# Unread products on TensorE around two waits, and four low weight parts moved from VectorE to GpSimd

## The chip, the cores and the metric

The kernel runs on one NeuronCore of a Trainium2 chip. The metric is the device time of one launch in microseconds, the median over runs. The engines are TensorE (PE, with its weight loads as PEld), VectorE (DVE), ScalarE (ACT), GpSimd (POOL) and SyncE (SP), which here only issues transfers. Each runs its own list of instructions in order; semaphores tie them together.

## The reference

The input is x of 4 batches by 512 tokens by 512 channels, in float32, and per batch a vector c.

```python
mod = silu(c) @ wmod                  # six rows: sa, ca, ga, sb, cb, gb
ga, gb = clamp_away_from_zero(ga), clamp_away_from_zero(gb)
h = layernorm(x) * (1 + ca) + sa
# mixer: causal depthwise convolution, B, C and delta projections,
# a linear scan over the 512 tokens with 128 states, output projection
x = x + ga * mixer(h)
h = layernorm(x) * (1 + cb) + sb
# experts: one of 2 for each token, the larger router logit wins
e = argmax(h @ w_router.T); p = softmax(h @ w_router.T)[e]
a = square(where(u >= 0, u, 0.5 * u)),  u = h @ w_fc[e].T    # 2048 hidden
x = x + gb * p * (a @ w_proj[e].T)
```

## The kernel before

**Mixer stage.** The batches b = 0 to 3 are worked through one after the other in a pipeline, with the order of every engine written out by hand. For each batch TensorE transposes the normalized rows (`transposes1`, L930, four column blocks k into two banks in turn), multiplies them by the delta, C, B and state weights (L937, L943, L951, L961) and makes the output (L978, L982). ScalarE normalizes, modulates (`modulate1`, L651, writes hT), adds the last tap of the convolution (L659) and takes the exponentials (eabs, L667 and L669). VectorE does the rest of the convolution (L1267), softplus, the scan, the residual and the statistics. Float32 products run on TensorE in full precision. Before all this TensorE multiplies the first modulation rows (`mod_rows`, L900) and turns them into columns by tiny transposes (`turn`, L916), and at the very start it runs two products of `ident` and `eabs` into the bank `pC` that nobody reads (L1013).

**Sorting.** While the mixer runs, each token gets a place in a list sorted by expert. VectorE finds the mask `m1` (L1343), TensorE counts with it (`prefix`, L987 and L988, two products of four columns), VectorE turns the counts into ranks, offsets and one-hot permutations (L1349 to L1362), GpSimd into positions (`positions`, L542 and L543, posI), and TensorE permutes the normalized tokens (`permuted_block`, L1006). ScalarE places each permuted block into the sorted activations (`place`, L729); of the last batch VectorE places a second copy (`place_from_back`, L1547). For the last batch (b = 3) there is no next batch whose products could stand between: TensorE has `permuted_block` of batch 2, then `prefix(3)`.

**Expert stage.** The 17 blocks of 128 sorted rows form five units of 4, 4, 4, 3 and 2 blocks. The hidden dimension is cut into eight parts hb; for each, TensorE computes for each unit the first product (`first_fc`, L1093, and `fc`, L1114) and the projection (`proj`, L1140). Both are split into a high and a low part in a faster float32 format: hi x hi, hi x lo and lo x hi are summed. So each weight chunk c (0 to 7 of each hb, 128x512; 0 to 3 for the first product, 4 to 7 for the projection) needs Whi (a copy on ScalarE, `split_first` L708 for hb = 0) and Wlo = raw - Whi, one subtraction of two SBUF tiles. The activations need XShi (ScalarE, `high_rows`, L819) and XSlo = XSfull - XShi (VectorE, `low_rows`, L1536, four operations for each unit, again with two SBUF inputs). Wlo comes from GpSimd (`low`, L547) for all chunks but the first four, which VectorE computes (`lows`, L1434). GpSimd waits for these before its first.

`first_fc` runs unit 0 in three passes: pass 0 (Whi, XShi), then the four permuted blocks of batch 3, then pass 1 (Whi, XSlo; it waits for the XSlo of each k) and pass 2 (Wlo, XShi; it waits for s_wlo >= 4). Then unit 1, all three passes.

Around the first expert products the orders are:

- VectorE: ranks(3), permutations(3), low_rows(0), lows(0 to 3), assign_rest (L1399 to L1404), low_rows(1), place_from_back(0 and 1), twice (L1554), place_from_back(2 and 3), alo (L1560).
- ScalarE: high_rows(0) and (1), margin_exp(3), place(3, blocks 0 and 1), split_first(4 to 7), the relu of unit 0 (L842), place(3, blocks 2 and 3), ahi and a_full (L851, L852).
- GpSimd: positions(3), the low parts 4 to 7, then the scatter of the sorted rows' metadata (L564).
- TensorE: first_fc of units 0 and 1, then `proj` of unit 0, which waits for alo.
- SyncE: loads the next raw weights when both s_whi and s_wlo have passed the chunks that they overwrite.

Of the kernel before, what the change touches and what calls it, by code (L numbers as in the profile page):

```python
# [17 lines left out]
F32 = mybir.dt.float32  # L18
# [3 lines left out]
ALU = mybir.AluOpType  # L22
# [25 lines left out]
CH = 8  # L48
# [48 lines left out]
def wait(eng, sem, count):  # L97

    if isinstance(count, int) and count <= 0:
        return  # L100
    eng.wait_ge(sem, count)


def build(nc, x, cT, wmod, wx, win, wout, conv_w, conv_b, A_log, Dvec, router_rows, wffn, out):
    with ExitStack() as ctx:
        base = (nc.sbuf_base + 63) // 64 * 64

        def at(name, shape, dt, offset):
            return nc.alloc_sbuf_tensor_at(name, shape, dt, offset=base + offset)

        def sem(name):
            return ctx.enter_context(nc.semaphore(name))
# [14 lines left out]
        raw = at("raw", [P, CH, 512], F32, o_raw)  # L127
        Whi = at("Whi", [P, 2, CH, 512], F32R, o_whi)
        Wlo = at("Wlo", [P, 2, CH, 512], F32R, o_wlo)
# [28 lines left out]
        def take(name, shape, dt=F32):  # L158
            o = cur[0]
            cur[0] += (int(np.prod(shape[1:])) * 4 + 31) // 32 * 32  # L160
            assert cur[0] <= limit[0], (name, cur[0] - limit[0])
            return at(name, shape, dt, o)
# [8 lines left out]
        eabs = take("eabs", [P, L])  # L171
# [26 lines left out]
        wout_sb = const("wout_sb", [P, DM])  # L198
        ident = const("ident", [P, P])
# [82 lines left out]
        pB, pC, pD, pX = bank[2:6]  # L282
# [105 lines left out]
        s_whi = sem("weights_hi_ready")  # L388
        s_wlo = sem("weights_lo_ready")
# [101 lines left out]
        def _(pool):  # L491
# [47 lines left out]
            def positions(b):  # L539
                pool.wait_ge(s_rk, b + 1)  # L540
                own.settle()
                own.link(pool.tensor_tensor(posF[:, :], pos[:, :], rank[:, :], ALU.subtract))  # L542
                pool.tensor_copy(posI[:, b % 2, :], posF[:, :]).then_inc(s_pos, 1)  # L543
# [6 lines left out]
            for b in range(NB):  # L550
                wait(pool, s_sc2[b % 2], 16 * TJ * (b // 2))
                pool.tensor_copy(meta[:, b % 2, :, 1:3].bitcast(I32), tokbat[:, TJ * b:TJ * b + TJ, :]).then_inc(s_tid, 1)
                candidates(b)
                positions(b)
                if b == NB - 1:

                    pool.wait_ge(s_wlo, CH // 2)
                    for c in range(CH // 2, CH):
                        low(0, c)
                pool.wait_ge(s_pos, b + 1)  # L560
                pool.wait_ge(s_tw, b + 1)
                pool.wait_ge(s_tid, b + 1)
                for j in range(TJ):
                    pool.indirect_dma_start(out=meta_dram, out_offset=bass.IndirectOffsetOnAxis(ap=posI[:, b % 2, j:j + 1], axis=0),  # L564
                                            in_=meta[:, b % 2, j, :], in_offset=None).then_inc(s_sc2[b % 2], 16)
# [322 lines left out]
        def _(pe):  # L888
# [15 lines left out]
            def turn(r):  # L904

                if r == 2:
                    pe.wait_ge(s_gar, 1)
                else:
                    pe.wait_ge(s_rw[r], 1)
                if r < 3:  # L910

                    wait(pe, s_cols, r)
                for k in range(KT):
                    o = KT * NB * (r % 3) + NB * k
                    row = gate_row if r == 2 else mod_row[r % 2]
                    mm = pe.transpose(col_bank[r][:, o:o + NB], row[:, P * k:P * k + P], ident[0:NB, 0:NB])  # L916
                mm.then_inc(s_mc, 1)

            def transposes1(b, ks=range(KT)):
                for k in ks:  # L920

                    wait(pe, s_e0, KT * (TJ * (b - 3) + k + 1))
                    if b == 2 and k < 2:

                        pe.wait_ge(s_cols, 3 + k)
                    wait(pe, s_hT, KT * b + k - 1)
                    for j in range(TJ):
                        if k == 0:
                            pe.wait_ge(s_z, TJ * b + j + 1)
                        mm = pe.transpose(pT[k % 2][:, P * j:P * j + P], z[b][:, j, P * k:P * k + P], ident[:, :])  # L930
                    mm.then_inc(s_zT, 1)

            def delta_product(b):
                wait(pe, s_dl, b)
                for k in range(KT):
                    pe.wait_ge(s_hT, KT * b + k + 1)
                    mm = pe.matmul(pD[:, :], wdb[:, k, :], hT[b % 2][:, k, PAD:PAD + L], start=(k == 0), stop=(k == KT - 1))  # L937
                mm.then_inc(s_pd, 1)
# [45 lines left out]
            def prefix(b):  # L984
                pe.wait_ge(s_m1, b + 1)
                pe.wait_ge(s_x2, TJ * (b + 1))
                pe.matmul(pO[0][:, 0:TJ], before[:, :], m1[:, :], start=True, stop=True).then_inc(s_pf, 1)  # L987
                pe.matmul(pO[0][:, TJ:2 * TJ], ones[:, :], m1[:, :], start=True, stop=True).then_inc(s_pf, 1)  # L988

            def permuted_block(b, j):  # L990
# [15 lines left out]
                    mm = pe.transpose(place_bank[b][j][:, P * k:P * k + P], z2[:, j, P * k:P * k + P], perm[:, j, :])  # L1006
                mm.then_inc(s_pz, 1)


            pe.wait_ge(s_const, 9)  # L1010
            pe.wait_ge(s_dconst, 1)
            for n in range(2):
                pe.matmul(pC[:, :], ident[:, :], eabs[:, :], start=True, stop=True)  # L1013
            pe.wait_ge(s_silu, 1)
            mod_rows(0)
            mod_rows(1)
            turn(0)
            transposes1(0, (0, 1))
            turn(1)
            transposes1(0, (2, 3))  # L1020
            pe.wait_ge(s_wdb, 1)
            delta_product(0)
# [7 lines left out]
            for b in range(NB):  # L1030
                nxt = b + 1 < NB
                for j in ORDER[:3]:
                    skip_product(b, j)
                if b == 0:
                    skip_product(b, 0)
                pe.wait_ge(s_hm, b + 1)
                pe.wait_ge(s_wg, b + 1)
                for j in ORDER[:3]:
                    state_output(b, j)
                if not nxt:  # L1040
                    permuted_block(b - 1, 0)
                    permuted_block(b - 1, 1)
                if b > 0:
                    skip_product(b, 0)
                state_output(b, 0)
                if not nxt:
                    permuted_block(b - 1, 2)
                    permuted_block(b - 1, 3)
                if b == 0:
                    delta_product(1)  # L1050
                    mod_rows(3)
                    mod_rows(4)
                    turn(3)
                elif nxt:
                    permuted_block(b - 1, 0)
                    permuted_block(b - 1, 1)
                if nxt:
                    C_product(b + 1)
                if b == 0:
                    turn(4)  # L1060
                if b == 1:
                    transposes1(b + 2, (0, 1))
                if nxt:
                    B_product(b + 1)
                if b == 0:
                    transposes1(b + 2, (0, 1))
                if b > 0 and nxt:
                    permuted_block(b - 1, 2)
                    permuted_block(b - 1, 3)
                if b == 2:  # L1070
                    mod_rows(5)
                if nxt:
                    state_product(b + 1)
                if b + 2 < NB:
                    transposes1(b + 2, (2, 3))
                    delta_product(b + 2)
                prefix(b)
            PARTS = ((0, 0), (0, 1), (1, 0))
            W, XS, A = (Whi, Wlo), (XShi, XSlo), (ahi, alo)

            def first_fc(u, parts):

                def body(e):
                    for n in parts:
                        wp, xp = PARTS[n]
                        if n == 2:
# [17 lines left out]
            def fc(par, hb, u):  # L1104
                i, w = NU * hb + u, P * UNITS[u]

                def body(pieces):
                    for m in range(HM):
                        for c0, c1, e in pieces:
                            n = 0  # L1110
                            for k in range(KT):
                                for wp, xp in PARTS:
                                    o = HB * (k % 2) + P * m
# [19 lines left out]
            def proj(par, hb, u):  # L1133
                i = NU * hb + u

                def body(experts):
                    for m in range(HM):
                        for s in range(UNITS[u]):
                            for n, (ap, wp) in enumerate(PARTS):
                                mm = pe.matmul(yP[s][:, :], A[ap][:, m, P * s:P * s + P], W[wp][:, par, 4 + 2 * experts[s] + m, :],  # L1140
# [82 lines left out]
        def _(dve):  # L1223
# [204 lines left out]
                dve.wait_ge(s_gbc, 16 * NB)  # L1428
                dve.tensor_tensor(woutg[b][:, :], wout_sb[:, :], ga_bc[:, b, :], ALU.mult).then_inc(s_wg, 1)

            def lows(cs):
                for c in cs:
                    dve.wait_ge(s_whi, c + 1)
                    dve.tensor_tensor(Wlo[:, 0, c, :], raw[:, c, :], Whi[:, 0, c, :].bitcast(F32), ALU.subtract).then_inc(s_wlo, 1)  # L1434

            own.mark(dve.memset(ones[:, :], 1.0))
            own.mark(dve.memset(run[:, :], 0.0))
            own.mark(dve.memset(hT[0][:, :, 0:PAD], 0.0))
# [44 lines left out]
            for b in range(NB):  # L1483
                nxt = b + 1 < NB
# [104 lines left out]
            ranks(NB - 1)  # L1589
            permutations(NB - 1)  # L1590
            low_rows(0)
            lows(range(4))
            assign_rest()
            low_rows(1)
            dve.wait_ge(s_e1, TJ * (NB - 1))
# [81 lines left out]
```

## Time and profile before

| | us |
|---|---|
| three runs | 555.43, 552.07, 554.42 |
| median | 554.42 |
| the profiled execution's own time | 554.07 |
| its span | 552.2 |

| engine | busy, us | share of the span |
|---|---|---|
| TensorE products | 508.4 | 92% |
| TensorE weight loads | 387.2 | 70% |
| VectorE | 345.8 | 63% |
| ScalarE | 261.2 | 47% |
| GpSimd | 149.8 | 27% |

The span is what the profiler recorded between the first and the last instruction; the time has 1.87 us more around it. All times of rows are from that one execution, counted from the start of its span. The mixer stage fills the first 150 us, the expert stage the rest. In the timeline a row is: start, length, engine, line, operation, output<-inputs, shape, count, and in brackets the idle time of that engine before it with what ended it. Float32 products appear as two records each (x8 is four products); records of one row overlap by a little, so a row's length over its count is not the time between starts. In the window rows stand the stretch, its length, TensorE's busy time and records in it, the granted clock as a share of 2.4 GHz (0.50 is 1.2 GHz; a value between means that the clock changed within the stretch), and the DMA engines' busy share with what they moved. In the chain's row "issue" is time in which the engine waited for nothing that the profile shows.

### The profile page before, as it was taken

Reading aid. Unit: us, or ns where it says so; the run is one execution under the profiler, and the core shown is the slowest. Engines: PE = TensorE matmul, PEld = TensorE weight load, DVE = VectorE, ACT = ScalarE, POOL = GpSimd, SP = SyncE. Lnnn points to the kernel's source line nnn. Section 1 sums busy time; section 2 is a strip of 40 time slices with the busy share of each in tenths; the row PEclk is TensorE's granted clock in tenths of the full one; section 3 lists DMA queues with packets and bytes.
Section 4 is the critical chain, followed back from the end, with each engine's and each line's share of the span. In section 5 each row is a group of like instructions: output and inputs, shape, how many; then the busy total and the mean of one; then the engine's idle time right before and its main releaser. Section 6 shows DMA issues by size and latency. Waiting matters only on the chain.

```text
span 552.2 us, 7695 instructions
## 1 busy us (share of the span) xinstructions
PE 508.4 (92%) x2280; PEld 387.2 (70%) x2280; DVE 345.8 (63%) x725; ACT 261.2 (47%) x520; POOL 149.8 (27%) x195
## 2 busy tenths in 40 slices
PE   6899899999388999999999999999999999999960
PEld 1345355544276888898888888889888888888840
DVE  4488999899999674554454545446444545446780
ACT  1664377957677633443443353344344335332310
POOL 1100003030335510330240042033015003734883
PEclk9899999999779999999999999999999999999995
DMA  8930351220043004220021022003002200344995
GB/s 303 425 113 0 113 194 57 97 77 2 1 129 103 4 3 154 69 87 1 1 87 69 1 78 78 1 23 134 1 1 77 78 2 0 85 112 93 155 125 66
DMA packets 15008, 44.19 MB, mean 80 GB/s; under 512 B 5016, under 2 KB 5016, under 8 KB 11624
## 3 DMA queue, kind: packets, MB, share of 16 engines
q1 hardware_dynamic: 10600, 34.71, 17.7%
q0 software_dynamic: 4352, 8.69, 8.9%
q8 instruction: 40, 0.66, 0.5%
q14 instruction: 16, 0.13, 0.1%
HBM read 34.94 MB, written 8.71 MB: 79 GB/s over the span
## 4 chain that ended last, share of the span: by engine, by line
PE 71%; DVE 17%; ACT 4%; issue 3%; DMA 1%; POOL 1%; ACTq 1%; SPq 0%; DVEq 0%; POOLq 0%
PE bank L1140 33%; PE bank L1114 32%; DVE xc L1267 4%; ACT XSfull L729 2%; DVE res L1305 2%; PE bank L937 1%; DVE st L1312 1%; DMA x_in<-x 1%; DVE st L1249 1%; POOL out L598 1%; DVE eabs L1329 1%; PE bank L1093 1%; DVE hs L1295 1%; PE bank L951 1%; PE bank L961 1%
## 5 line engine op out<-in xcount | busy, mean ns | idle before, releaser
L547 POOL TENSOR_TENSOR Wlo<-raw,Whi (+1 forms) x60 | 76.2, 1300 | 233.8 <-ACT Whi L857 225.2
L1570 DVE TENSOR_TENSOR acc<-acc,bank 128x512 f32<-128x512 f32 x119 | 81.2, 687 | 62.6 <-PE bank L1140 62.6
L1554 DVE TENSOR_TENSOR twice_h<-twice_h,bank 128x512 f32<-128x512 f32 (+2 forms) x80 | 48.1, 606 | 99.2 <-ACT twice_h L842 99.2
L1140 PE MATMUL bank<-Whi,ahi 128*128 128x512 f32 x272 | 106.1, 390 | 3.7 <-DVE alo L1560 3.7
L1114 PE MATMUL bank<-XShi,Wlo 128*128 x304 | 108.1, 355 | 0.0
L1114 PE MATMUL bank<-XSlo,Whi 128*128 x304 | 108.0, 355 | 0.0
L1114 PE MATMUL bank<-XShi,Whi 128*128 x304 | 108.0, 355 | 0.0
L1140 PE MATMUL bank<-Wlo,ahi 128*128 128x512 f32 x272 | 106.1, 390 | 0.0
L1140 PE MATMUL bank<-Whi,alo 128*128 128x512 f32 x272 | 106.0, 390 | 0.0
L851 ACT ACTIVATE ahi<-twice_h 128x512 fp32r<-128x512 f32 (+2 forms) x80 | 45.5, 568 | 120.3 <-PE bank L1140 120.3
L842 ACT ACTIVATE twice_h<-bank 128x512 f32<-128x512 f32 (+2 forms) x80 | 42.2, 531 | 87.0 <-PE bank L1114 77.7
L1114 PEld LDWEIGHTS bank<-XShi,Whi 128*128 128x128 f32 x304 | 57.3, 189 | 7.5
L1114 PEld LDWEIGHTS bank<-XSlo,Whi 128*128 128x128 f32 x304 | 57.3, 188 | 7.5
L1114 PEld LDWEIGHTS bank<-XShi,Wlo 128*128 128x128 f32 x304 | 57.3, 189 | 6.9
L1140 PEld LDWEIGHTS bank<-Whi,ahi 128*128 128x128 f32 x272 | 51.1, 188 | 14.6 <-issue 4.5
L1140 PEld LDWEIGHTS bank<-Whi,alo 128*128 128x128 f32 x272 | 51.1, 188 | 10.7
L1140 PEld LDWEIGHTS bank<-Wlo,ahi 128*128 128x128 f32 x272 | 51.1, 188 | 10.1
L1560 DVE TENSOR_TENSOR alo<-a_full,ahi 128x512 fp32r<-128x512 f32 (+2 forms) x80 | 46.2, 607 | 0.0
L852 ACT ACTIVATE a_full<-twice_h 128x512 f32<-128x512 f32 (+2 forms) x80 | 44.2, 552 | 0.0
L1267 DVE SCALAR_TENSOR_TENSOR xc<-hT,cw,xc 128x512 f32<-128x512 f32 x48 | 33.6, 743 | 1.8 <-ACT xc L659 1.4
L729 ACT ACTIVATE XSfull<-bank,cols 128x128 f32 (+1 forms) x64 | 24.1, 457 | 17.1 <-PE bank L1006 15.4
L598 POOL DMA_INDIRECT out<-acc,sorted_meta x17 | 28.2, 1659 | 12.2 <-DVE acc L1578 8.2
(182 smaller groups left out, 552.3 us busy)
## 6 DMA issues: line engine op xcount, KB each, us to landing
raw<-wffn SPq DMA_DIRECT2D x16, 1024.0 KB, 5.2
wm<-wmod SPq DMA_DIRECT2D x6, 1024.0 KB, 12.5
out<-res SPq DMA_DIRECT2D x4, 1024.0 KB, 4.5
x_in<-x SPq DMA_DIRECT2D x3, 1024.0 KB, 12.4
ga_bc<-ga_rows SPq DMA_DIRECT2D x4, 256.0 KB, 3.7
x<-x SPq DMA_DIRECT2D x1, 1024.0 KB, 5.3
bc<-router_rows_scaled SPq DMA_DIRECT2D x4, 256.0 KB, 3.5
wx_sb<-wx SPq DMA_DIRECT2D x1, 514.0 KB, 8.5
```

The source lines that it names most:

```text
L547: pool.tensor_tensor(Wlo[:, hb % 2, c, :], raw[:, c, :], Whi[:, hb % 2, c, :].bitcast(F32), ALU.subtract).then_inc(s_wlo, 1)
L598: pool.indirect_dma_start(out=out, out_offset=bass.IndirectOffsetOnAxis(ap=sorted_meta[:, n, 1:2].bitcast(I32), axis=0), in_=acc[:, n, :], ...
L729: act.activation(XSfull[:, k, bass.ds(first, P)], place_bank[b][j][:, P * k:P * k + P], ACT.Identity, bias=cols[:, 4, k, b:b + 1], scale=c ...
L842: act.activation(twice_h[:, m, 0:w], hP[(par + u) % 2][m][:, 0:w], ACT.Relu).then_inc(s_relu[m], 1)
L851: act.activation(ahi[:, m, 0:w], twice_h[:, m, 0:w], ACT.Square, scale=0.5).then_inc(s_ah[m], 1)
L852: act.activation(a_full[:, m, 0:w], twice_h[:, m, 0:w], ACT.Square, scale=0.5).then_inc(s_af[m], 1)
L1114: mm = pe.matmul(hP[(par + u) % 2][m][:, c0:c1], W[wp][:, par, 2 * e + k // 2, o:o + P], XS[xp][:, k, bass.ds(start_row[u] + c0, c1 - c0)] ...
L1140: mm = pe.matmul(yP[s][:, :], A[ap][:, m, P * s:P * s + P], W[wp][:, par, 4 + 2 * experts[s] + m, :], start=(m == 0 and n == 0), stop=(m = ...
L1267: ins = dve.scalar_tensor_tensor(xc[:, b % 2, k, :], hT[b % 2][:, k, tap:tap + L], cw[:, k, tap:tap + 1], xc[:, b % 2, k, :], ALU.mult, AL ...
L1554: dve.tensor_tensor(twice_h[:, m, 0:w], twice_h[:, m, 0:w], hP[(par + u) % 2][m][:, 0:w], ALU.add).then_inc(s_q2[m], 1)
L1560: dve.tensor_tensor(alo[:, m, 0:w], a_full[:, m, 0:w], ahi[:, m, 0:w].bitcast(F32), ALU.subtract).then_inc(s_al2[m], 1)
L1570: dve.tensor_tensor(acc[:, n, :], acc[:, n, :], yP[s][:, :], ALU.add).then_inc(s_yu, 1)
```

## The change

Three edits. TensorE gets a helper `idle_products(n, operand)` that multiplies `ident` by an operand of 512 columns into the bank `pC`, which nobody reads; the two such products at the start now use it. One product is added between turn(1) and the transposes of columns 2 and 3 of batch 0, four before and two behind the prefix counts of the last batch. And VectorE's four low parts of the first expert weights (`lows`) are gone: GpSimd computes all eight, right behind positions(3), without its wait for VectorE's.

```diff
--- before.py
+++ after.py
@@ -553,9 +553,7 @@
                 candidates(b)
                 positions(b)
                 if b == NB - 1:
-
-                    pool.wait_ge(s_wlo, CH // 2)
-                    for c in range(CH // 2, CH):
+                    for c in range(CH):
                         low(0, c)
                 pool.wait_ge(s_pos, b + 1)
                 pool.wait_ge(s_tw, b + 1)
@@ -1006,17 +1004,21 @@
                     mm = pe.transpose(place_bank[b][j][:, P * k:P * k + P], z2[:, j, P * k:P * k + P], perm[:, j, :])
                 mm.then_inc(s_pz, 1)
 
+            def idle_products(n, operand):
+
+                for _ in range(n):
+                    pe.matmul(pC[:, :], ident[:, :], operand[:, :], start=True, stop=True)
 
             pe.wait_ge(s_const, 9)
             pe.wait_ge(s_dconst, 1)
-            for n in range(2):
-                pe.matmul(pC[:, :], ident[:, :], eabs[:, :], start=True, stop=True)
+            idle_products(2, eabs)
             pe.wait_ge(s_silu, 1)
             mod_rows(0)
             mod_rows(1)
             turn(0)
             transposes1(0, (0, 1))
             turn(1)
+            idle_products(1, eabs)
             transposes1(0, (2, 3))
             pe.wait_ge(s_wdb, 1)
             delta_product(0)
@@ -1074,7 +1076,11 @@
                 if b + 2 < NB:
                     transposes1(b + 2, (2, 3))
                     delta_product(b + 2)
+                if not nxt:
+                    idle_products(4, wout_sb)
                 prefix(b)
+                if not nxt:
+                    idle_products(2, wout_sb)
             PARTS = ((0, 0), (0, 1), (1, 0))
             W, XS, A = (Whi, Wlo), (XShi, XSlo), (ahi, alo)
 
@@ -1427,11 +1433,6 @@
             def out_weights(b):
                 dve.wait_ge(s_gbc, 16 * NB)
                 dve.tensor_tensor(woutg[b][:, :], wout_sb[:, :], ga_bc[:, b, :], ALU.mult).then_inc(s_wg, 1)
-
-            def lows(cs):
-                for c in cs:
-                    dve.wait_ge(s_whi, c + 1)
-                    dve.tensor_tensor(Wlo[:, 0, c, :], raw[:, c, :], Whi[:, 0, c, :].bitcast(F32), ALU.subtract).then_inc(s_wlo, 1)
 
             own.mark(dve.memset(ones[:, :], 1.0))
             own.mark(dve.memset(run[:, :], 0.0))
@@ -1589,7 +1590,6 @@
             ranks(NB - 1)
             permutations(NB - 1)
             low_rows(0)
-            lows(range(4))
             assign_rest()
             low_rows(1)
             dve.wait_ge(s_e1, TJ * (NB - 1))
```

## Rows read from the trace of the kernel before

**Rows 1.** The chain that ended last, by engine.

```profile
PE 71%; DVE 17%; ACT 4%; issue 3%; DMA 1%; POOL 1%; ACTq 1%; SPq 0%; DVEq 0%; POOLq 0%
```

**Rows 2.** Timeline of TensorE, first stretch.

```profile
17.38 0.40 PE L916 MATMUL bank<-ident,mod_row 4*128 4x4 f32 x4
18.87 1.78 PE L930 MATMUL bank<-ident,z 128*128 128x128 f32 x8 [1.08 <-ACT hT L651]
20.44 4.80 PE L937 MATMUL bank<-hT,wdb 128*128 128x512 f32 x8
...
49.02 3.60 PE L937 MATMUL bank<-hT,wdb 128*128 128x512 f32 x8
```

**Rows 3.** Windows: PE busy (x), PEclk, DMA share, GB/s.

```profile
145.50:146.00 0.50, 0.00 (x0) 0.73 0.00 0
159.00:159.50 0.50, 0.50 (x4) 0.61 0.68 82
...
19.40:19.60 0.20, 0.19 (x3) 0.60 1.07 451
...
22.80:23.00 0.20, 0.20 (x2) 0.87 1.08 451
```

**Rows 4.** Timeline of ScalarE, first stretch.

```profile
22.11 1.52 ACT L659 ACTIVATE xc<-hT,cb,cw 128x512 f32<-128x512 f32 x2
25.28 0.60 ACT L667 ACTIVATE eabs<-bank 128x512 f32<-128x512 f32 x1 [1.65 <-PE bank L937]
```

**Rows 5.** Timeline of TensorE, start of the expert stage.

```profile
149.85 0.59 PE L987 MATMUL bank<-m,before 128*128 128x4 f32 x2 [6.59 <-DVE m L1343]
...
153.26 3.77 PE L1093 MATMUL bank<-XShi,Whi 128*128 x8 [2.39 <-ACT XShi L819]
156.84 3.16 PE L1006 MATMUL bank<-perm,z 128*128 128x128 f32 x16
...
163.49 1.98 PE L1093 MATMUL bank<-XShi,Whi 128*128 x8
...
171.09 0.50 PE L1140 MATMUL bank<-Whi,ahi 128*128 128x512 f32 x1 [2.00 <-DVE alo L1560]
```

**Rows 6.** Timeline of ScalarE, start of the expert stage.

```profile
158.02 1.50 ACT L729 ACTIVATE XSfull<-bank,cols 128x128 f32 x4 [2.24 <-PE bank L1006]
...
161.11 2.20 ACT L708 ACTIVATE Whi<-raw 128x512 fp32r<-128x512 f32 x4
...
166.37 1.51 ACT L729 ACTIVATE XSfull<-bank,cols 128x128 f32 x4 [0.20 <-ACT XSfull L729]
```

**Rows 7.** Timeline of VectorE, start of the expert stage.

```profile
153.49 2.50 DVE L1536 TENSOR_TENSOR XSlo<-XSfull,XShi  x4
155.91 2.49 DVE L1434 TENSOR_TENSOR Wlo<-raw,Whi 128x512 fp32r<-128x512 f32 x4
...
159.84 2.50 DVE L1536 TENSOR_TENSOR XSlo<-XSfull,XShi  x4 [0.54 <-issue]
...
168.02 1.37 DVE L1547 TENSOR_SCALAR XSfull<-bank,cols 128x128 f32 x4 [0.34 <-ACT XSfull L729]
169.31 1.36 DVE L1560 TENSOR_TENSOR alo<-a_full,ahi 128x512 fp32r<-128x512 f32 x2
```

**Rows 8.** Timeline of GpSimd, its last positions.

```profile
153.00 0.29 POOL L543 CAST posI<-posF 128x4 int32<-128x4 f32 x1
```

**Rows 9.** Timeline, narrow windows: XSlo (VectorE) and low parts (GpSimd) at one time.

```profile
161.89 1.60 POOL L547 TENSOR_TENSOR Wlo<-raw,Whi 128x512 fp32r<-128x512 f32 x1 [8.60 <-ACT Whi L708]
...
182.78 1.30 POOL L547 TENSOR_TENSOR Wlo<-raw,Whi  x1
...
183.71 0.79 DVE L1536 TENSOR_TENSOR XSlo<-XSfull,XShi  x1
...
193.66 1.47 POOL L547 TENSOR_TENSOR Wlo<-raw,Whi  x1
...
193.90 1.51 DVE L1536 TENSOR_TENSOR XSlo<-XSfull,XShi  x1
```

## Prediction

> **What bounds the kernel now.** First the page's chain that ended last [rows 1]: TensorE holds 71% of it and VectorE 17%. From 171.09 us on TensorE computes the expert products with hardly a gap, so what can be won lies before that point: whatever moves the first projection product (L1140, 171.09) moves the end by as much. So I read the two stretches that the change touches, engine by engine in the timeline, and the granted clock in narrow windows over them.
>
> The first transposes [rows 2]: after the small transposes of L916 (until 17.8) TensorE waits 1.08 us for hT. At about 19.44 its clock falls to 1.2 GHz and is back at 2.4 GHz at about 22.85 [rows 3]. In that time the delta product takes 4.80 us; the same product at 2.4 GHz takes 3.60. ScalarE waits for it: its row of eabs shows 1.65 us idle [rows 4].
>
> The last prefix count [rows 5]: TensorE idles 6.59 us before it, the clock falls at about 145.7 and returns only at about 159.4 [rows 3]. So the eight products of L1093 at 153.26 take 3.77 us (eight like them take 1.98 at 2.4 GHz, at 163.49), and the 16 transposes of L1006 take 3.16 us. ScalarE places the first block at 158.02 after 2.24 us idle, and then works nearly without a wait to 167.88 [rows 6]. VectorE waits 0.34 us for that at 168.02, ends alo at 170.67 [rows 7], and TensorE goes on at 171.09, after 2.00 us idle. VectorE is the second bound of this stretch: from 153.49 to 170.67 it waits for little but that 0.34.
>
> **Part one, one product between turn(1) and the second pair of transposes.** It costs about 0.9 us at 2.4 GHz (3.60 for four [rows 2]), starts at 17.8 and ends at 18.7, before 18.87, so it is hidden by the wait for hT; were the clock low already it would take 1.8 and cost 0.7. I take it that the clock then holds. The delta product is then bound by ScalarE's last two hT pieces, ends near 23.4, and eabs starts when ScalarE has finished its last taps, 23.65 instead of 25.28. VectorE had been waiting for eabs too, so everything behind moves: **-1.6 us**. Ends: +0.7 and -1.6 (ScalarE is busy until 23.63 [rows 4], more can't come).
>
> **Part two, four products before and two after the last prefix count.** The last transposes end at 143.27, so the four take until 146.8 at 2.4 GHz; 3.0 us of waiting are left. m1 comes from VectorE at 149.8, so nothing waits for them (at 1.2 GHz they would end 0.3 us past it, and VectorE fills that time with z2 before it reads the counts). The clock held over the 2.00 us before 171.09 and fell within the 6.59 us; 3.0 us and the small counts lie between. I expect a fall, but a return several us before 159.4, since TensorE is then busy from 149.85 on. The two products behind the count end at 152.2 at 2.4 GHz, or 154.3 at 1.2 GHz, 1.05 us past the 153.26 at which XShi is there. Placement on ScalarE could so start between 156.0 (its own end of high_rows and the margin's exponential) and 159.1, against 158.02; I take 157.0. By itself, with the placement as the bound, this would be worth -1.0 us, ends -2.0 and +1.05. It decides nothing if the next part is as I think.
>
> **Part three, the first four low parts on GpSimd.** Removed from VectorE: 2.49 us at 155.91 [rows 7]. Added on GpSimd: four of 1.29 us. GpSimd is free after posI at 153.29 [rows 8] and the Whi that they need was split before the count, so they start at about 153.33, beside VectorE's XSlo rows (four of 0.68 us, 153.49 to 155.99), and not alone. What happens then the trace shows in three places [rows 9]:
> - VectorE's XSlo at 183.71 (384 columns; the next one took 0.55) took 0.79 and ended at 184.50, 0.42 after GpSimd's low part had ended at 184.08.
> - XSlo at 193.90 (256 columns, 0.41 alone) took 1.51: it sat through GpSimd's whole low part of 193.66 to 195.13 and ended 0.28 after it. That low part had itself taken 1.47.
> - GpSimd's low part at 161.89 took 1.60 beside the fourth XSlo of unit 1, which ended at about 162.34; without one it takes 1.29.
>
> So operations with two SBUF inputs on the two engines run one after the other, in turns, and each starts 0.13 us before the other's recorded end (195.41-0.41=195.00 against 195.13; 163.49-1.29=162.20 against 162.34). A turn of one low part and one XSlo of 512 columns is thus 1.29+0.68-2x0.13=1.71 us, where an XSlo alone follows the last in 0.60. First batch: the first low part ends 154.62, the first XSlo 155.17, the fourth 155.17+3x1.71=**160.3** instead of 155.99. The low parts are ready at 159.75, so it is XSlo that TensorE waits for. It needs 13 more products of 0.23: h is ready at 163.4, about as before, whatever part two gained.
>
> VectorE then needs 1.44 us (assign_rest and the load of a register, 158.40 to 159.84 in rows 7) and begins XSlo of unit 1 at 161.7 instead of 159.84. GpSimd's other four low parts started at 161.89, when only the last XSlo was left; they follow ScalarE's Whi at 161.11 [rows 6], with part two a little earlier, so at 160.9. Now all four XSlo meet them: the first ends 162.7 (162.2-0.13+0.68), the fourth 162.7+3x1.71=**167.9** instead of 162.34.
>
> From there VectorE had 8.33 us to the end of alo, 0.3 of it waits: 167.9+8.0=175.9, and TensorE's first projection 0.4 later, 176.3 instead of 171.09: **+5.2 us**. Ends: if the engines don't get into each other's way, VectorE gains 2.5, ScalarE's placement is the bound and this part costs 0; if each waits for the other's recorded end the turn is 1.97, and eight turns make it +7.3. I take the middle value, since three overlaps of three fit it.
>
> The Trainium skill ("SBUF — State Buffer", section on who interferes with whom) has this as a rule: a VectorE instruction with two SBUF inputs contends with a GpSimd one that reads SBUF, and the one that issues later blocks for the whole instruction. Taken literally it gives the turn of 1.97 us and a time 2.1 us above mine; the rows above show the 0.13 us of overlap, so the measurement decides.
>
> **The clock behind it.** TensorE ends the products of unit 1 at about 167.9+13x0.23=171.0 and waits 5.3 us for the projection, where it waited 2.00. The clock fell within the 6.59 us wait, so I expect 1.2 GHz at 176.3. After the two falls of the trace TensorE worked at 1.2 GHz for 3.4 us (from 19.44) and 6.1 us (153.26 to 159.4); half of that is lost: **+2.4 us** (1.7 to 3.1; 0 if the clock holds).
>
> **Sum.** -1.6+5.2+2.4=+6.0 on the profiled execution's 554.07 (span 552.2 and 1.87 around it), which is 0.35 below the median of the three runs: 560.1 us.
>
> **Rivals.**
> (a) GpSimd and VectorE don't hold each other up here. For: only three overlaps are there to judge by, none with four operations queued on either side. Against: all three are slowed, and by one and the same rule of time. Then the placement is the bound: -1.6-1.0, and 0.5 more or less: 551.5 us, faster. It decides if XSlo at 153.5 keeps its 0.68. Chance 0.17.
> (b) Only the first batch collides, because GpSimd's second four come when XSlo of unit 1 is over, as they do now. VectorE then is +4.3-2.49-0.34=+1.5 late, TensorE waits 3.5 us, the clock perhaps holds: 554.0, with a fall 556.4. Against: XSlo of unit 1 moves 1.9 us later, and ScalarE's Whi does not. Chance 0.13.
> (c) The collision as forecast, but the clock holds over the 5.3 us: 557.7. For: it held over 2.00. Chance 0.1.
> (d) The added products don't keep the clock up at 19.4, either since one is too few or since it comes at another moment in each execution: 1.6 more than each case. It moves with the spread of the three runs (552.07 to 555.43) and is in the range. Chance 0.2 across all cases.
> Forecast: 0.6.
>
> **The numbers.** A measurement of this kernel tells about 1% from no change, 548.9 to 560.0. The forecast's own range is 558.0 to 562.5, its upper end with the turn of 1.97 us. A little over half of its 0.6 lies above 560.0, which is 0.34; (d) lifts the rest of it and (c) past that bound for another 0.12: slower 0.46. Faster by over 1% needs (a) with every gain at its end: 0.04. The rest, 0.5, is within 1%. The range leaves out part of (a): 552.3 to 562.7.
>
> **What would show it.** Right: XSlo rows at about 152 (all times 1.6 us earlier there) of 1.4 to 1.7 us instead of 0.68, twice four of them; low parts of 1.7 us; TensorE's wait before the first L1140 over 4 us and a granted clock of 0.50 behind it; delta product near 3 us and full clock at 19 to 23; full clock before 159. Wrong: XSlo at 0.68 beside running low parts breaks part three; the low clock still at 19.4 breaks part one; a first L1140 ahead of 171 breaks the forecast.

## The result and the profile after

The changed kernel takes 559.73 us (median of 4 runs, 558.81 to 560.65), the kernel before 553.29 in the same comparison (552.07 to 555.43). The ratio is 1.0106, 95% interval 1.0073 to 1.0138: slower by 1.1%. The profiled execution took 558.81 us, the fastest of the four; its span is 557.1. One execution of the kernel before that ran beside e5 to e8 took 1336 us and is left out of their ratios.

The first stretch of TensorE and ScalarE, to be held against [rows 2, 4]:

```profile
17.10 0.41 PE L914 MATMUL bank<-ident,mod_row 4*128 4x4 f32 x4
17.44 1.13 PE L1010 MATMUL bank<-eabs,ident 128*128 128x512 f32 x2
18.59 1.33 PE L928 MATMUL bank<-ident,z 128*128 128x128 f32 x8
19.75 3.60 PE L935 MATMUL bank<-hT,wdb 128*128 128x512 f32 x8
```

```profile
23.39 0.60 ACT L665 ACTIVATE eabs<-bank 128x512 f32<-128x512 f32 x1
```

The product fills the wait, the delta product takes 3.60 us instead of 4.80, and eabs starts at 23.39 instead of 25.28 (0.28 of that came with x, which landed earlier in this execution).

TensorE at the start of the expert stage [rows 5], and its granted clock (columns as in [rows 3]):

```profile
141.23 3.60 PE L1010 MATMUL bank<-wout_sb,ident 128*128 128x512 f32 x8
148.00 0.59 PE L985 MATMUL bank<-m,before 128*128 128x4 f32 x2 [3.17 <-DVE m L1349]
...
148.87 3.76 PE L1010 MATMUL bank<-wout_sb,ident 128*128 128x512 f32 x4
151.64 3.48 PE L1099 MATMUL bank<-XShi,Whi 128*128 x8
154.96 1.91 PE L1004 MATMUL bank<-perm,z 128*128 128x128 f32 x16
...
158.49 1.42 PE L1099 MATMUL bank<-XSlo,Whi 128*128 x5 [0.93 <-DVE XSlo L1537]
...
166.54 1.61 PE L1099 MATMUL bank<-XSlo,Whi 128*128 x5 [1.20 <-DVE XSlo L1537]
...
174.94 0.79 PE L1146 MATMUL bank<-Whi,ahi 128*128 128x512 f32 x1 [3.60 <-DVE alo L1561]
```

```profile
147.00:147.50 0.50, 0.00 (x0) 0.57 0.00 0
153.50:154.00 0.50, 0.50 (x2) 0.60 0.00 0
167.50:168.00 0.50, 0.50 (x3) 0.55 0.85 279
170.50:171.00 0.50, 0.50 (x3) 0.53 0.00 0
174.00:174.50 0.50, 0.00 (x0) 0.88 0.00 0
174.50:177.50 3.00, 2.56 (x6) 0.50 0.00 0
177.50:178.00 0.50, 0.50 (x3) 0.71 0.06 4
```

The clock falls at about 147.1 and is back at 153.9, 5.5 us earlier than in the kernel before (1.9 of it because everything up to m1 is earlier), and the 16 transposes take 1.91 us instead of 3.16. But now TensorE waits for XSlo within the first products, and the first projection comes at 174.94 instead of 171.09, with the clock at 1.2 GHz from 174.4 until 177.8. The clock is also at 1.2 GHz from 167.5 to 171.0, within the last products of unit 1. They take 3.40 us for that (1.98 in the kernel before), but end at 171.3, ahead of alo at 174.5, so this costs nothing.

Why is on VectorE and GpSimd, to be held against [rows 7, 8]:

```profile
151.64 6.71 DVE L1537 TENSOR_TENSOR XSlo<-XSfull,XShi  x4
...
159.99 6.41 DVE L1537 TENSOR_TENSOR XSlo<-XSfull,XShi  x4 [0.73 <-issue]
...
173.23 1.29 DVE L1561 TENSOR_TENSOR alo<-a_full,ahi 128x512 fp32r<-128x512 f32 x2
```

```profile
151.39 6.41 POOL L547 TENSOR_TENSOR Wlo<-raw,Whi 128x512 fp32r<-128x512 f32 x4
159.48 6.37 POOL L547 TENSOR_TENSOR Wlo<-raw,Whi 128x512 fp32r<-128x512 f32 x4 [1.69 <-ACT Whi L706]
```

Two fours of XSlo took 2.50 us each; now they take 6.71 and 6.41, beside two fours of low parts that take 6.4 us where four without company take 5.05 (e5). One turn of the two engines, from a narrow window:

```profile
154.37 1.74 POOL L547 TENSOR_TENSOR Wlo<-raw,Whi 128x512 fp32r<-128x512 f32 x1
...
154.89 1.77 DVE L1537 TENSOR_TENSOR XSlo<-XSfull,XShi  x1
```

The low part ends at 156.11, the XSlo 0.55 later at 156.66; the next pair begins at 156.07 and 156.59, 1.70 us after this one.

### The profile page after: what moved, and what is told of

It is laid out like the page before. It is cut to its first block, busy times and chain, and to the rows that moved or that the text cites. A ratio compares the mean times of both kernels' runs of the same rounds, so it can differ in the third digit from the quotient of the medians.

```text
span 557.1 us, 7722 instructions
## 1 busy us (share of the span) xinstructions
PE 516.7 (93%) x2294; PEld 389.5 (70%) x2294; DVE 351.7 (63%) x721; ACT 261.5 (47%) x520; POOL 157.2 (28%) x199
## 4 chain that ended last, share of the span: by engine, by line
PE 70%; DVE 20%; issue 4%; ACT 2%; DMA 1%; POOL 1%; DVEq 1%; SPq 0%; ACTq 0%; POOLq 0%
PE bank L1146 33%; PE bank L1120 32%; DVE xc L1273 4%; DVE res L1311 2%; DVE st L1318 1%; DVE XSlo L1537 1%; PE bank L935 1%; DMA x_in<-x 1%; DVE st L1255 1%; POOL out L596 1%; DVE eabs L1335 1%; DVE XSfull L1548 1%; DVE hs L1301 1%; PE bank L949 1%; PE bank L959 1%
## 5 line engine op out<-in xcount | busy, mean ns | idle before, releaser
L547 POOL TENSOR_TENSOR Wlo<-raw,Whi (+1 forms) x64 | 83.6, 1333 | 228.3 <-ACT Whi L855 226.6
```

Of the source, the lines that this page charges most:

```text
L547: pool.tensor_tensor(Wlo[:, hb % 2, c, :], raw[:, c, :], Whi[:, hb % 2, c, :].bitcast(F32), ALU.subtract).then_inc(s_wlo, 1)
```

## The experiments

Twelve more kernels ran. Each has one profiled execution; where that one isn't near its kernel's median, the text says so. Ratios are to the kernel before on the same chip (median 554.61 us for the first eight, 553.88 for the last four).

**The parts alone: e1, e2, e3.** e1 has all seven products with VectorE's low parts back, e2 only the moved low parts, e3 only the first product.

```diff
 e1                                     e2
+lows(range(4))          # VectorE     -idle_products(1, eabs)
+pool.wait_ge(s_wlo, CH // 2)          -idle_products(4, wout_sb)
-for c in range(CH):                   -idle_products(2, wout_sb)
+for c in range(CH // 2, CH):
 e3: as e1, and
-idle_products(4, wout_sb)
-idle_products(2, wout_sb)
```

Expected of e1: 

> All seven added products, but the first four low parts back on VectorE, with GpSimd's wait for them. Collision theory: the products are not what makes the changed kernel slow; XSlo takes 0.68 us again, the first L1140 comes 1.6 to 2.0 us earlier than in the kernel before, and the time is 0.995 to 0.998 of it. Rival (the products stand in TensorE's way, or keep it busy when m1 comes): the time stays at or above 1.005 of the kernel before.

Expected of e2: 

> None of the seven products, only the four low parts moved to GpSimd. Collision theory: all eight XSlo operations of units 0 and 1 but at most two take 1.6 to 1.8 us, the first L1140 comes 5.2 us later than in the kernel before, and with the cold clock behind it the time is 1.011 to 1.015 of it, more than the changed kernel's 1.0106. Rival (moving work off VectorE, which is nearly always busy in this stretch, helps or is neutral): at or below 1.000.

Expected of e3: 

> Of the whole change only the one product ahead of the second pair of transposes. If it holds the clock at 19.4 us: granted clock 1.00 from 15 to 25 us, delta product 3.6 us, eabs 1.6 us earlier, time 0.997 of the kernel before. If the clock's fall is a matter of each execution's chance: the median moves by half of that or less.

| run | median, us | ratio | 95% interval |
|---|---|---|---|
| e1 products only | 557.63 (553.23 to 558.38) | 1.0028 | 0.9996 to 1.0061 |
| e2 low parts only | 560.67 | 1.0096 | 1.0065 to 1.0127 |
| e3 one product | 554.74 | 0.9990 | 0.9962 to 1.0018 |

e2 carries the whole loss. Its XSlo rows are 6.72 and 5.97 us long, and its first projection comes at 176.24, 5.15 us after that of the kernel before (forecast 5.2). The time is below the 1.011 to 1.015 expected of it, and it isn't above the changed kernel's.

```profile
153.23 6.72 DVE L1532 TENSOR_TENSOR XSlo<-XSfull,XShi  x4
...
161.73 5.97 DVE L1532 TENSOR_TENSOR XSlo<-XSfull,XShi  x4 [0.87 <-issue]
```

e3 holds the clock and starts eabs early in its profile (23.74 us), but its median doesn't differ from the kernel before. The profile is of the fastest of its ten executions. Four took 552.85 to 553.26 us with a mean granted clock of 0.974, the other six 554.51 to 556.52 with 0.972 or 0.973; at which moment the clock was lower in those isn't recorded. The expected 0.997 lies within the interval, and so does no change.

e1 was a miss for the collision theory as I had applied it. Its profile shows XSlo of unit 0 at 2.50 us, and this:

```profile
158.42 5.79 DVE L1544 TENSOR_TENSOR XSlo<-XSfull,XShi  x4 [0.54 <-issue]
```

```profile
158.82 6.54 POOL L547 TENSOR_TENSOR Wlo<-raw,Whi 128x512 fp32r<-128x512 f32 x4 [6.95 <-ACT Whi L708]
```

The earlier clock lets TensorE permute earlier, ScalarE place and split Whi earlier (158.03 instead of 161.11), and so GpSimd's four low parts, which always were its own, start 0.4 us behind the first XSlo of unit 1. In the kernel before only the last XSlo met them. The first projection is at 172.74, 1.65 us behind that of the kernel before, after a wait of 5.17 us, and the clock is at 1.2 GHz until 176.4. The span is 4.0 us longer, so 2.35 of it comes behind the first projection. Against the kernel before, the interval of e1's ratio still includes no change. Against e3, on the same chip with ten executions each, the median is 2.9 us and the mean 2.2 us higher: a faster TensorE at this place, and a longer kernel.

**The same products with one wait more: e5, e6.**

```diff
+pool.wait_ge(s_xlo, 2 * KT)    # GpSimd, ahead of low(0, 4)
```

e5 is e1 with it, e6 the changed kernel with it.

Expected of e5: 

> The seven products with the low parts as in the kernel before, and one more wait: GpSimd begins low parts 4 to 7 only when the four XSlo of unit 1 are done. Collision theory: in the products-only kernel the earlier clock lets ScalarE's Whi, and so GpSimd's second four, begin 0.4 us behind the first XSlo of unit 1, and that alone made it slow; with the added wait XSlo takes 0.68 us each, the first L1140 comes before 169.5 us, and the time falls from 1.003 to 0.994 to 0.997 of the kernel before. Rival (the products themselves cost, on TensorE or through the clock): a wait more on GpSimd can't make it faster, it stays at 1.003 or above.

Expected of e6: 

> The changed kernel with that same wait ahead of low parts 4 to 7. Collision theory: the first four XSlo still take 1.7 us each, the second four 0.68; the first L1140 comes 3.9 us earlier than in the changed kernel, near 171.0 us, TensorE's wait before it is near 2 us; time 1.001 to 1.004 of the kernel before, against 1.0106. Rival (the delay comes from the first batch alone, or from what GpSimd does, whenever it does it): 1.008 to 1.012 as before.

e5: 554.08 us, ratio 0.9968 (0.9941 to 0.9995), where e1 had 1.0028. e6: 555.73 us, 1.0000 (0.9971 to 1.0028), where the changed kernel has 1.0106. By the medians a wait added to GpSimd takes away 3.6 and 4.0 us. The kernels of each pair ran on different chips, but the intervals of their ratios don't overlap, those of e1 and e5 only just. In e5's profile XSlo of unit 1 is back at 2.50 us and the first projection is at 169.24. In e6 VectorE shows the first collision alone:

```profile
151.92 6.71 DVE L1539 TENSOR_TENSOR XSlo<-XSfull,XShi  x4
160.34 2.50 DVE L1539 TENSOR_TENSOR XSlo<-XSfull,XShi  x4 [0.81 <-issue]
```

and its first projection is at 171.37 (expected 171.0), 3.6 us ahead of the changed kernel's. That settles that the coincidence costs, not the amount of work on GpSimd.

**Low parts where VectorE reads PSUM or takes statistics: e4, e7.** Both are the changed kernel with parts 0 to 3 ahead of the scatter of batch 2; e7 has a wait for the first residual of batch 3.

```diff
 pool.wait_ge(s_tid, b + 1)
+if b == NB - 2:
+    pool.wait_ge(s_x2, TJ * (NB - 1) + 1)    # e7 alone
+    for c in range(CH // 2):
+        low(0, c)
```

Expected of e4: 

> The changed kernel, but GpSimd computes low parts 0 to 3 ahead of the scatter of batch 2, at about 137 to 143 us, when VectorE adds residuals from PSUM and takes statistics, operations with one SBUF input. Collision theory: no XSlo of unit 0 is held up (0.68 us each), unit 1's are over before GpSimd's second four begin, VectorE is 2.5 us ahead and ScalarE's placement becomes the bound: 2.6 us below the kernel before, 0.994 to 0.997. Rival (it is not the coincidence but that GpSimd is slower at this work, or late with what stands behind it in its queue): the time stays above 1.003, since GpSimd has as much to do as in the changed kernel and its scatter comes 5 us later.

Expected of e7: 

> The kernel with low parts 0 to 3 ahead of the scatter of batch 2, with a wait of GpSimd for the first residual of batch 3 before them. In the first form of it two operations of VectorE with eight columns (limits) took 1.25 and 1.20 us beside the low parts instead of 0.23 and 0.17. Theory: they have a form that needs what GpSimd holds, and with the wait none of VectorE's operations there is held up; m1 comes 2.0 us earlier and the median is 550.8 to 551.8, 0.991 to 0.994. Rival (the later scatter, or GpSimd being late for the positions of batch 3, takes it back): m1 is earlier but the median stays at 553.

e4: 553.07 us, 0.9955 (0.9928 to 0.9982). The profile is of the slowest of its eleven executions (555.78 us). Its XSlo rows are back at 2.50 us each, but m1 is 2.0 us late, because two tiny operations met low parts. The narrow window on one of them:

```profile
136.83 1.29 POOL L547 TENSOR_TENSOR Wlo<-raw,Whi 128x512 fp32r<-128x512 f32 x1 [1.84 <-DVE meta L1378]
136.91 1.25 DVE L1403 TENSOR_SCALAR limits<-blkF,rows_in_front 128x8 f32<-128x8 f32 x1
```

Eight columns, 1.25 us. e7: **551.91 us, 0.9943 (0.9915 to 0.9971)**, 0.1 us above the range expected of it. The profile is of its fastest execution (550.23 us). Here the limits take 0.22 and 0.17 again and both fours of XSlo 2.50, and ScalarE's placement bounds VectorE (0.34 us of wait before its last placement):

```profile
138.19 4.96 POOL L547 TENSOR_TENSOR Wlo<-raw,Whi 128x512 fp32r<-128x512 f32 x4 [3.32 <-DVE res L1315]
139.29 0.70 DVE L1322 BATCH_NORM_STATS2 st<-res 128x6 f32<-128x512 f32 x1
139.90 0.67 DVE L1315 TENSOR_TENSOR res<-bank,x 128x512 f32<-128x512 f32 x1
...
155.89 2.50 DVE L1541 TENSOR_TENSOR XSlo<-XSfull,XShi  x4 [0.54 <-issue]
...
164.52 1.36 DVE L1552 TENSOR_SCALAR XSfull<-bank,cols 128x128 f32 x4 [0.34 <-ACT XSfull L731]
```

Beside the low parts VectorE's residual (one operand in a PSUM bank) takes 0.67 us and its statistics 0.70, as in e6 without low parts there, and four low parts take 4.96. The first projection is at 167.59, 3.5 us before that of the kernel before. e7 is faster than both kernels: the same edits, with the low parts at another moment.

**What exactly is held up: e10, e11**, a single execution each. In e10 GpSimd clears the first four low parts, in e11 VectorE writes XSlo of units 0 and 1 from one input.

```diff
 e10
+pool.memset(Wlo[:, 0, c, :].bitcast(F32), 0.0)      # c = 0 to 3
 e11
+dve.tensor_scalar(XSlo[...], XSfull[...], 0.0, None, ALU.mult)    # u < 2
```

Expected of e10: 

> The changed kernel, but GpSimd only clears the first four low parts (a memset, which reads nothing): the low weights of the first product are left out for hb = 0. If the collision is over reading SBUF: the first XSlo that overlaps with a memset takes 0.68 us, no XSlo of unit 0 takes longer. If any GpSimd operation of such a size holds VectorE up: up to 1.7 us as before.

Expected of e11: 

> The changed kernel, but VectorE's XSlo of units 0 and 1 are written by a tensor_scalar of XSfull alone, times zero: one SBUF input, so the low activations of these units are left out for hb = 0. GpSimd's low parts stay as they are. If only a second SBUF input is held up: each takes 0.68 us or less beside a low part. If the two blocked operations of VectorE in the run with early low parts (tensor_scalar too, 1.25 and 1.20 us) show that this form is held up as well: 1.3 us and more, in turns with the low parts. The Trainium skill (SBUF - State Buffer, section on who interferes with whom) names tensor_scalar among the operations that may take both ports and contend.

e10: the four XSlo take 2.50 us (151.81 to 154.31) beside memsets of 0.52 to 0.60, the time is 550.03. In the rows the first of them and the permutation ahead of it, a tensor_scalar, stand beside a memset:

```profile
151.48 1.14 DVE L1371 TENSOR_SCALAR perm<-colidx,place_col 128x128 f32<-128x128 f32 x1
151.55 0.52 POOL L558 MEMSET Wlo<- 128x512 f32 x1
...
151.81 0.81 DVE L1540 TENSOR_TENSOR XSlo<-XSfull,XShi  x1
...
151.81 2.50 DVE L1540 TENSOR_TENSOR XSlo<-XSfull,XShi  x4
```

The permutation's row is 1.14 us long where it takes 0.28 elsewhere. But XSlo begins 0.33 us behind its start, as it does in the changed kernel (151.31 and 151.64), so VectorE lost no time to it. This row doesn't show whether a tensor_scalar and a memset hold each other up.

e11: the one-input form is held up as well, and when alone it is the faster one:

```profile
151.77 5.65 DVE L1538 TENSOR_SCALAR XSlo<-XSfull  x4
...
158.85 1.43 DVE L1538 TENSOR_SCALAR XSlo<-XSfull  x4 [0.53 <-issue]
```

So VectorE's subtraction of two SBUF tiles collides with a GpSimd subtraction that reads SBUF (6.71 us for four) and not with a memset, which only writes (2.50), and a tensor_scalar with one SBUF input collides with the subtraction too (5.65 instead of 1.43). The Trainium skill ("SBUF — State Buffer", section on who interferes with whom) states this division for two SBUF inputs, and has tensor_scalar among the operations that can take both ports; the three cases here agree.

**The clock behind the longer wait: e8, e9.** Both add unread products ahead of the first projection of the changed kernel, into the bank of unit 0's h. e8 has three behind the waits for the placements, e9 four ahead of them.

```diff
+for m in range(HM):
+    pe.wait_ge(s_q2[m], 1)
+for _ in range(4):                 # e8: 3, and behind the wait for s_e1d
+    pe.matmul(bank[0][:, :], ident[:, :], wout_sb[:, :], start=True, stop=True)
```

Expected of e8: 

> The changed kernel with three more unread products between the first products of unit 1 and the first projection, into the bank of unit 0's h once VectorE has read it. If the cold clock behind the longer wait costs what the profile shows (2.7 us of work at 1.2 GHz from 174.9 on), the clock stays at 2.4 GHz there and the time is 1.3 us (0.2%) below the changed kernel. If the wait alone matters and the clock does not: no change against 559.7.

Expected of e9: 

> The changed kernel with four unread products ahead of the first projection, this time before TensorE waits for the placements, so that they start once VectorE's twice of unit 0 is done (170.5 us) and end before alo (174.5). If the cold clock costs what the changed kernel's profile shows: granted clock 1.00 from the first projection on, 1.3 us less than the changed kernel, 558.4. If the clock does not matter there: 559.7 and more.

e8: 560.51 us, 1.0095 (1.0058 to 1.0131). The products stood behind a wait that ended at 173.1; the clock fell at 174.0, they took 4.5 us, most of it at 1.2 GHz, and the projection began at 176.71, 2.3 us after it could. So e8 doesn't answer its question: the clock wasn't held. e9: 557.12 us, 1.0063 (1.0039 to 1.0087), clock 1.00 from 170 us on, first projection at 174.15. That is more than the 1.3 us expected, but e9's profiled execution also had two of GpSimd's second four done before XSlo of unit 1 began (4.04 us instead of 6.41). The two profiles divide it: e9's span is 2.2 us shorter, 0.8 of it ahead of the first projection and 1.4 behind it (380.75 us from there to the end, against 382.16 in the changed kernel). The other profiles agree in kind. With the full clock from the first projection to 180 us that rest is 380.75 to 381.42 us (the kernel before, e3, e7, e9, e10, e12), with 1.2 GHz for a part of it 382.09 to 383.46 (the changed kernel, e1, e2, e4, e5, e6, e8, e11).

**e12**, e7 with seven products ahead of the prefix count instead of four.

Expected of e12: 

> The kernel with early low parts behind the added wait (551.9 us) with seven products instead of four ahead of the last prefix count; they end at 147.8, before m1 at 148.3. If the clock's fall behind the four still costs: granted clock 1.00 from 141 to 165 us, placement of the first block 0.8 us earlier at most (ScalarE is busy until 154.2), median 0.3 to 0.8 us lower. If ScalarE's and VectorE's own work sets the pace by now: no change.

551.20 us, 0.9948 (0.9929 to 0.9966): the granted clock is 1.00 from 144 to 156 us, TensorE waits 1.38 us for XShi, and ScalarE places the first block at 154.82, 0.19 earlier than in e7 (the profiled execution took 550.11 us). The ratio can't be told from e7's: the clock is no longer what counts there.

## Why the prediction was right

559.73 us against 560.1 forecast. The collision, which decides the sign, came step by step as forecast; that the sum is so near is in part luck. The forecast was +6.0 us on the profiled execution. Profile against profile it is +4.7, median against median +6.4. In medians the two other terms were both too large, with opposite signs: e2, with part three and the clock, is 6.1 us above the kernel before where 5.2 and 2.4 were forecast, and e3, with part one, shows none of its -1.6 for certain.

- **Part three.** The turn of a low part and an XSlo was to be 1.71 us; it is 1.70. First four to take 6.81 us, took 6.71; second four to take 6.2, took 6.41. e2 puts the first projection 5.15 us later, forecast 5.2. The reading of each overlap from recorded ends (0.13 us before the other's end) was better than the turn of 1.97 us. e6 shares the loss out: 3.6 us of the first projection (4.0 by the medians) are the second four's, which rival (b) had left out; e6's 555.73 lies in that rival's span of 554.0 to 556.4. Rival (a), no collision, fell with the first profile.
- **Part one.** -1.6 us: in the profile 1.61 (25.28 to 23.39, less the 0.28 of x). In the medians it can't be seen: e3 at 0.9990. Rival (d) keeps its weight: one profile of each kernel shows when the clock fell, and of the other executions only the mean clock is recorded. Six of e3's ten were slower than its profile by 1.7 us and more, at a lower mean clock.
- **Part two.** "It decides nothing if the next part is as I think" held for the changed kernel, but "by itself, with the placement as the bound, this would be worth -1.0 us" was wrong. Alone, the six products cost 2.9 us (medians of e1 and e3, 557.63 and 554.74), since they move GpSimd's second four into XSlo of unit 1. I had followed ScalarE's Whi to GpSimd for part three and not for part two by itself. The clock's fall behind the four products and its early return came as forecast. How much of the 5.5 us is the products' stays open: the clock came back between 152.0 and 157.1 us in ten profiles with them, and without them at 155.8 (e2), 157.5 (e3) and 159.4 (the kernel before).
- **The clock behind.** Right in kind, too large in size: forecast +2.4 (1.7 to 3.1). The first projection is 3.85 us late and the span 4.9 longer, which leaves 1.05; at 1.2 GHz TensorE worked 2.9 us. The wait was 3.60 us and not the 5.3 forecast, since the clock had fallen once before, within unit 1's products, which the forecast didn't have. It was taken from two earlier stretches of 3.4 and 6.1 us; the return comes at a moment of its own, and here it came soon.
- A sum of 3.6 for the first projection (5.2 less 1.6) stands against 3.85 measured (4.1 without the 0.28 us of x); the clock's term is what left the profile at 558.81 instead of 560.1.

## To carry to other kernels

Before work moves from VectorE to GpSimd, look at what VectorE does in the same microseconds: where both read two SBUF tiles, they take turns, and each of VectorE's short operations pays most of GpSimd's long one (1.1 us of 1.29 here). The cure is a moment, not a split: put GpSimd's operations beside VectorE's reads of PSUM and its statistics, with a wait if need be (e7; e5 and e6 show what the wait alone gives). And a faster engine can move a third engine's start into a collision, so unread products that hold TensorE's clock must be followed as far as GpSimd.

## What the runs showed that I had not expected

- A tensor_scalar of eight columns took 1.25 us beside a GpSimd subtraction, while memsets leave four two-input tensor_tensor of 512 columns at 2.50.
- Six products that bring the clock back earlier made the kernel longer (e1 against e3), and one wait added on GpSimd gave 3.6 us back (e5).
- Unread products issued after the wait that they should fill, not in it, cost 2.3 us ahead of the projection (e8), although the clock is then back soon.
- The kernel before spreads from 553.0 to 559.2 us over 31 executions on one chip. Where the clock returns moves the start of GpSimd's second four: in the changed kernel, e8 and e9, which are alike up to there, it returns at 153.9, 156.9 and 152.5 us, the four start at 159.48, 160.25 and 158.41, and alo at 173.23, 172.67 and 172.45. Whether this makes the spread of the kernel before isn't shown.
